# Probabilities times values: products of 64 rows for each sequence of a pair, one PSUM bank for each

## The chip, the cores and the metric

The kernel runs on one core of a Trainium2 chip. Times are device microseconds (us) of one execution; the time of a kernel is the median of its runs.

## What is computed

A gated cross-attention layer and a gated mixture of low-rank experts, on 32 sequences of 64 tokens of width 512. The part that the change touches is attention; the layer's reference, cut:

```python
x = x + jnp.tanh(g_xattn[0]) * attention(_layernorm(x), ctx, ctx, mask, wq, wk, wv, wo)
# attention, per sequence b (64 tokens), 32 query heads, 8 key/value heads of width 128
q, k = _apply_rope(query @ wq), _apply_rope(key @ wk)
v = value @ wv
raw = jnp.einsum('bhqd,bhkd->bhqk', q, k) / scale
attn = jax.nn.softmax(raw + mask, axis=-1)
out = jnp.einsum('bhqk,bhkd->bhqd', attn, v)
return out @ wo
```

The product `attn` times `v` is a sum over the 64 tokens of one sequence: half of the 128 rows of TensorE's array.

## The kernel before

Everything is one program in which each engine's order of instructions is written out by hand; semaphores connect the engines. First 64 products make keys and values of all sequences (line 839, with the layer norm of x beside them) and keep them in DRAM. Then come 64 steps (`STEPS`). A step is four sequences (`SUB_SEQS`, two pairs, `PAIRS`) with the four query heads (`GROUP`) that share one key/value head. The last four steps (`WIDE` on) are written out apart, because there are no more query projections to fill TensorE; the work of the experts (lines 811, 983, 1008, 1012) fills steps from 30 on and the end.

Precision: a float32 operand is split into a high part, rounded to the type fp32r, and a low part, the rest. A product is then three products of fp32r, high by high, low by high and high by low (`SPLIT_PRODUCTS`). Scores (line 894) are plain float32, and each such product leaves two matmul records in the trace.

TensorE's order in a step of the main loop (k from 1 to 59) is: scores of step k; `times_values(k-1)`; two query projections (`product`, line 877, six matmuls of 512 columns each); `project_out(k-1, 0)` (line 945, twelve matmuls of 512 columns); a further projection in every second step, and `turn_probs(k)`, which turns the probabilities of step k (line 905); `project_out(k-1, 1)`; one more projection.

`times_values` is what changes. It works on a pair of sequences at a time. The probabilities, turned, have the tokens of the pair on the 128 rows (sequence A on rows 0 to 63, B on 64 to 127) and head and query on the 512 columns, 256 to a pair. For each pair, into one bank (`attn[bp]`), with A's result on columns 0 to 255 and B's on 256 to 511, it issues (lines 930, 932):

- for each of the two sequences ("twins") one matmul of all 128 rows and 256 columns. `v_s[:, twin]` holds that sequence's high values on one half of the rows and its low values on the other, and `p_high[:, twin]` its high probabilities on both halves, so one matmul gives two of the three products;
- one matmul of 128 rows and 512 columns for the third product: `v_both` (high values of both) by `p_low`, a block-diagonal tile with zeros where a sequence meets the other's columns.

So a step has 6 matmuls and 6 weight loads for values, with 4 x 256 + 2 x 512 = 2,048 columns. ScalarE makes `p_high` with two copies out of PSUM (line 1621) and two copies to the other half of the rows (line 1624). VectorE makes `p_low` with two subtractions of 64 rows (line 1262). GpSimd writes the zeros of `p_low` once (line 1892). The SP queue fetches values for two steps at a time with four transfers to `v_s` and one to `v_both` (lines 649, 651).

Who waits for whom: `times_values` waits for `probs_low` and `probs_high`, for the values (`v_in`), and, for each bank, until `add_out` (line 1282, VectorE) has added that bank's earlier output projection to `acc` (semaphore `x1_added`). Each of its two banks raises `values_used` at its own last matmul. On that, `attn_high` (line 1633, ScalarE) and `attn_low` (line 1270, VectorE) split the bank into `o_s`, for which `project_out` waits.

Of the kernel before, what the change touches and what calls it, by code (L numbers as in the profile page):

```python
# [8 lines left out]
F32 = mybir.dt.float32  # L9
# [4 lines left out]
P = 128  # L14
# [29 lines left out]
TWIN_ROWS = (slice(0, SEQ), slice(SEQ, 2 * SEQ))  # L44

# [150 lines left out]
FOUR_UNTIL, ZEROS_BESIDE = 63, 63  # L196
# [96 lines left out]
def build(nc, x, ctx, mask, g_attn, g_ffn, wq, wk, wv, wo, routed_w, lora_b, table, out):  # L293
# [8 lines left out]
    with ExitStack() as stack:  # L302
# [28 lines left out]
        p_high = sb_at(base + 73728, "p_high", [P, 2, 512], F32R)  # L331
# [8 lines left out]
        p_low = sb_at(base + 131072, "p_low", [P, PAIRS, 2, GROUP * SEQ], F32R)  # L340
# [26 lines left out]
        v_both = sb("v_both", [P, 2, CHUNK_TILES, DH], F32R)  # L367
# [64 lines left out]
        zeros_set, warm_zeros = sem("zeros_set"), sem("warm_zeros")  # L432
# [130 lines left out]
        def _(e):  # L563
# [71 lines left out]
            def fetch_values(u):  # L635
                G, c, index = chunk_of(u)
                g = G % KV_HEADS
                if u >= 2:
                    e.wait_ge(values_used, PAIRS * SUBS * (u - 1))
                else:  # L640
                    e.wait_ge(x_low, 4 * len(X_PAIRS))
                if u == 0 or u == 1 or G == KV_HEADS:
                    for slot in range(VST):
                        e.wait_ge(v_stored[slot], 32 * len(range(slot, len(V_NO), VST)))
                cols = slice(g % 4 * DH, g % 4 * DH + DH)
                for twin in range(2):
                    for part in range(2):
                        rows = TWIN_ROWS[twin if part == 0 else 1 - twin]
                        e.dma_start(v_s[rows, u % 2, twin, :, :].bitcast(F32),
                                    v_kept[index, g // 4, part, TWIN_ROWS[twin], :, cols]).then_inc(v_in[u % 2], 16)  # L650
                e.dma_start(v_both[:, u % 2, :, :].bitcast(F32), v_kept[index, g // 4, 0, :, :, cols]).then_inc(v_in[u % 2], 16)
# [149 lines left out]
        def _(e):  # L801
# [79 lines left out]
            def scores(k):  # L881
                u, s = divmod(k, SUBS)
                G, c, index = chunk_of(u)
                e.wait_ge(rope_added, ROPE_NO["q", HEAD_PAIRS * G + 1, 1 if c == 0 else 3] + 1)
                e.wait_ge(k_in[u % 2], 16 * (u // 2 + 1))
                if k:
                    e.wait_ge(masked, k)
                free(score)
                for hp in range(HEAD_PAIRS):
                    for b in range(SUB_SEQS):  # L890
                        seq = s * SUB_SEQS + b
                        col = (hp * SUB_SEQS + b) * SEQ
                        two_heads = q_r[Q_SLOT[G, hp, c]][:, seq, :, :].rearrange("p h s -> p (h s)")
                        last = e.matmul(score[:, col:col + SEQ], two_heads, k_r[:, u % 2, seq * SEQ:(seq + 1) * SEQ],  # L894
                                        start=True, stop=True)
                last.then_inc(scored, 1)

            def turn_probs(k):
# [8 lines left out]
                drained[turned.name] = probs_low, 2 * k + 2  # L907

            def times_values(k, pairs=range(PAIRS)):
                u, s = divmod(k, SUBS)  # L910
                tiles = [s * PAIRS + bp for bp in range(PAIRS)]
                e.wait_ge(v_in[u % 2], 80 * (u // 2 + 1))
                e.wait_ge(probs_low, 2 * k + 2)
                e.wait_ge(probs_high, 3 * k + 3)
                cols = [slice(bp * GROUP * SEQ, (bp + 1) * GROUP * SEQ) for bp in range(PAIRS)]
                for bp in pairs:
                    if k == 0:

                        e.wait_ge(rope_added, ROPE_NO[JOBS[bp - PAIRS]] + 1)
                    elif k + 1 == STEPS:  # L920

                        if bp == 0:
                            e.wait_ge(masked, STEPS)
                        else:
                            e.wait_ge(x1_added, 2 * k - 1)
                    else:
                        e.wait_ge(x1_added, 2 * k - 1 + bp)
                    b = out_bank(k, bp)
                    for twin in range(2):
# [19 lines left out]
            def expert(what, t):  # L949
# [15 lines left out]
                elif what == "route":  # L965
# [8 lines left out]
                    elif t >= HALF_TILES + 2:  # L974

                        e.wait_ge(probs_low, 2 * STEPS)
# [113 lines left out]
            times_values(k + 1, [0])  # L1090
            scores(k + 3)
            times_values(k + 1, [1])
# [41 lines left out]
        def _(e):  # L1134
# [119 lines left out]
            def prob_low(k, *twins):  # L1254
                for twin in twins:
                    rows = TWIN_ROWS[twin]
                    e.wait_ge(probs_high, 3 * k + twin + 1)
                    if k:
                        e.wait_ge(values_used, PAIRS * k)
                    else:  # L1260
                        e.wait_ge(zeros_set, 1)
                    e.tensor_tensor(p_low[rows, :, twin, :], turned[rows, :].rearrange("p (b n) -> p b n", b=PAIRS),  # L1262
                                    p_high[rows, twin, :].bitcast(F32).rearrange("p (b n) -> p b n", b=PAIRS),
                                    ALU.subtract).then_inc(probs_low, 1)
# [134 lines left out]
            prob_low(0, 0, 1)  # L1399
            finish_key(len(JOBS) - 1)  # L1400
            for k in range(1, WIDE):
# [30 lines left out]
                if not together:  # L1432
                    prob_low(k, 0)
# [4 lines left out]
                prob_low(k, *((0, 1) if together else (1,)))  # L1438
# [25 lines left out]
            prob_low(k, 0, 1)  # L1464
# [6 lines left out]
            prob_low(k + 1, 0, 1)  # L1471
# [11 lines left out]
            prob_low(k + 2, 0, 1)  # L1483
# [9 lines left out]
            prob_low(k + 3, 0, 1)  # L1493
# [28 lines left out]
        def _(e):  # L1522
# [92 lines left out]
            def prob_high(k):  # L1615
# [184 lines left out]
        def _(e):  # L1800
# [80 lines left out]
            for n in range(len(JOBS)):  # L1881
# [7 lines left out]
                if n == ZEROS_BESIDE:  # L1889

                    e.wait_ge(rope_added, FOUR.stop)
                    e.memset(p_low[:, :, :, :].bitcast(F32), 0.0).then_inc(zeros_set, 1)
# [139 lines left out]
```

## Time and profile before

| | us |
|---|---|
| median of 3 runs (1090.81 to 1091.05) | 1091.02 |
| span of the profiled execution, first to last instruction | 1089.0 |
| TensorE matmul busy in it | 1082.4 (99%) |
| TensorE weight load busy | 919.3 (84%) |
| VectorE busy | 874.1 (80%) |
| ScalarE busy | 636.8 (58%) |
| GpSimd busy | 591.9 (54%) |

The own time of the profiled execution is not given beside its span; the median is 2.0 us above the span, which is what lies around it. Busy time of TensorE is time in which at least one matmul is under way, from its start to its modelled end. Matmuls overlap, so what a matmul costs is read from the distance of starts, not from its own duration.

### The profile page before, as it was taken

What the parts mean: (1) busy time and instruction counts of PE and PEld (TensorE: products, weight loads), DVE (VectorE), ACT (ScalarE), POOL (GpSimd) and SP (SyncE); (2) the same over time, 40 slices, a digit from 0 to 9 for tenths busy, and PEclk for the clock granted to TensorE, in tenths of its full rate; (3) what the DMA queues carried; (4) which work ended last, traced back from release to release, by engine and by line L of the source; (5) the groups of instructions that cost most, each with busy time, mean ns of one, the idle gap of its engine ahead of it and who ended that gap; (6) DMA issues with size and microseconds to landing.
All of it is one profiled execution on the core that took longest, in us unless ns stands there. A gap on an engine that the chain in (4) does not pass through costs nothing.

```text
span 1089.0 us, 17107 instructions
## 1 busy us (share of the span) xinstructions
PE 1082.4 (99%) x5640; PEld 919.3 (84%) x5640; DVE 874.1 (80%) x1423; ACT 636.8 (58%) x1112; POOL 591.9 (54%) x518
## 2 busy tenths in 40 slices
PE   9999999999999999999999999999999999999998
PEld 7888888888888888888888888888888888888886
DVE  7876657888888888888887898777777777777887
ACT  7563476586666666666655545555555555555553
POOL 5552379888877777777754433333333333333423
PEclk9999999999999999999999999999999999999999
DMA  7858964496646464646489546553535353543112
GB/s 258 273 210 336 391 220 183 155 379 201 214 155 213 155 213 156 212 156 212 141 300 380 185 136 205 177 187 111 187 110 187 112 184 114 179 116 118 40 39 78
DMA packets 106087, 206.27 MB, mean 189 GB/s; under 512 B 8849, under 2 KB 58641, under 8 KB 100113
## 3 DMA queue, kind: packets, MB, share of 16 engines
q1 hardware_dynamic: 105424, 204.40, 55.2%
q8 instruction: 47, 0.77, 0.3%
q10 hardware_dynamic: 576, 0.79, 0.2%
q14 instruction: 40, 0.32, 0.1%
HBM read 122.31 MB, written 82.84 MB: 188 GB/s over the span
## 4 chain that ended last, share of the span: by engine, by line
PE 97%; DVE 2%; DMA 0%; issue 0%; ACT 0%; DVEq 0%; SPq 0%
PE attn L945 32%; PE proj L877 28%; PE score L894 10%; PE attn L839 8%; PE score L839 4%; PE turned L839 4%; PE attn L930 3%; PE attn L932 3%; PE turned L905 3%; PE proj L811 1%; PE small L983 1%; PE small L1008 1%; PE score L983 0%; DMA near_raw<-in_ctx 0%; DVE o_s L1270 0%; DVE stats L1140 0%
## 5 line engine op out<-in xcount | busy, mean ns | idle before, releaser
L945 PE MATMUL attn<-wo_s,o_s 128*128 128x512 f32 x1524 | 374.7, 395 | 0.2 <-DVE o_s L1270 0.2
L877 PE MATMUL proj<-xB,wq_s 128*128 128x512 f32 x1344 | 332.6, 391 | 0.0
L945 PEld LDWEIGHTS attn<-wo_s,o_s 128*128 128x128 f32 x1524 | 280.9, 188 | 57.0 <-DVE o_s L1270 0.4
L877 PEld LDWEIGHTS proj<-xB,wq_s 128*128 128x128 f32 x1344 | 252.0, 188 | 51.3 <-issue 0.2
L1863 POOL TENSOR_TENSOR rot<-rot,tab 128x512 f32<-128x512 f32 x110 | 162.3, 1475 | 145.2 <-ACT rot L1584 145.0
L1633 ACT ACTIVATE o_s<-attn 128x512 fp32r<-128x512 f32 x127 | 69.3, 595 | 112.2 <-PE attn L932 112.1
L894 PEld LDWEIGHTS score<-k_r,q_r 128*128 128x128 f32 x1024 | 123.9, 191 | 5.5 <-DVE q_r L1180 0.4
L1175 DVE TENSOR_TENSOR q_r<-q_r,tab 128x512 f32<-128x512 f32 x127 | 120.9, 952 | 1.5 <-ACT x_third L1584 1.4
L894 PE MATMUL score<-k_r,q_r 128*128 128x64 f32 x1024 | 121.3, 271 | 0.0
L1605 ACT ACTIVATE copies<-proj 128x512 f32<-128x512 f32 x96 | 57.5, 599 | 78.0 <-PE proj L877 77.8
L1282 DVE SCALAR_TENSOR_TENSOR acc<-attn,gates_t,acc 128x512 f32<-128x512 f32 x127 | 94.8, 747 | 4.1 <-PE attn L945 1.2
L1863 POOL TENSOR_TENSOR rot_third<-rot_third,tab 128x512 f32<-128x512 f32 x40 | 61.3, 1533 | 57.6 <-ACT rot_third L1584 54.8
L1262 DVE TENSOR_TENSOR p_low<-turned,p_high 64x512 fp32r<-64x512 f32 x128 | 87.7, 686 | 5.2 <-ACT p_high L1621 2.8
L1621 ACT ACTIVATE p_high<-turned 64x512 fp32r<-64x512 f32 x128 | 75.6, 590 | 23.5 <-PE turned L905 21.8
L1583 ACT ACTIVATE rot<-q_r 64x512 f32<-64x512 f32 x84 | 52.4, 623 | 52.5 <-DVE q_r L1219 51.4
L1270 DVE TENSOR_TENSOR o_s<-attn,o_s 128x512 fp32r<-128x512 f32 x127 | 81.4, 680 | 1.8 <-ACT o_s L1633 1.7
L1624 ACT ACTIVATE p_high<-p_high 64x512 fp32r<-64x512 f32 x128 | 80.8, 631 | 2.8
L1219 DVE TENSOR_TENSOR q_r<-copies,proj 128x512 f32<-128x512 f32 x127 | 81.1, 678 | 0.3 <-issue 0.3
L1180 DVE TENSOR_TENSOR q_r<-q_r,rot 128x512 f32<-128x512 f32 x85 | 69.2, 814 | 6.0 <-POOL rot L1863 0.3
L1241 DVE SCALAR_TENSOR_TENSOR prob_odd<-score,mask_sb 128x512 f32<-128x512 f32 x32 | 22.1, 691 | 52.7 <-PE score L894 52.6
L1870 POOL TENSOR_TENSOR prob_odd<-prob_odd,neg_max 128x512 f32<-128x512 f32 x32 | 33.7, 1053 | 54.9 <-DVE neg_max L1246 54.0
L1870 POOL TENSOR_TENSOR prob_even<-prob_even,neg_max 128x512 f32<-128x512 f32 x32 | 33.5, 1047 | 48.5 <-DVE neg_max L1246 48.5
(269 smaller groups left out, 1681.5 us busy)
## 6 DMA issues: line engine op xcount, KB each, us to landing
wq_kept<-wq_s SPq DMA_DIRECT2D x16, 1792.0 KB, 6.3
wq_s<-wq_kept SPq DMA_DIRECT2D x16, 1792.0 KB, 8.2
v_kept<-vst SPq DMA_DIRECT2D x64, 256.0 KB, 4.3
v_s<-v_kept SPq DMA_DIRECT2D x128, 128.0 KB, 5.0
wo_kept<-wo_s SPq DMA_DIRECT2D x32, 512.0 KB, 5.7
wo_s<-wo_kept SPq DMA_DIRECT2D x32, 512.0 KB, 5.2
k_kept<-kst SPq DMA_DIRECT2D x32, 256.0 KB, 2.2
wq_raw<-in_wq SPq DMA_DIRECT2D x16, 512.0 KB, 7.8
```

The source lines that it names most:

```text
L839: last = e.matmul(b[:, :], stationary, moving, start=(kt == 0 and m == 0), stop=(kt == KT - 1 and m == 2))
L877: last = e.matmul(dst[:, :], wq_s[:, b % 2, A, s, kt, :], xB[:, B, mv, kt, :], start=(first and kt == 0 and m == 0), stop=(kt == 1 and m = ...
L894: last = e.matmul(score[:, col:col + SEQ], two_heads, k_r[:, u % 2, seq * SEQ:(seq + 1) * SEQ], start=True, stop=True)
L945: last = e.matmul(out_bank(k, bp)[:, :], o_s[:, s, bp, h, :], wo_s[n % WO_SLOTS][:, m, :], start=(h == 0 and i == 0), stop=(h == GROUP - 1 ...
L1175: e.tensor_tensor(dst, src, cos, ALU.mult).then_inc(times_cos, 1)
L1219: e.tensor_tensor(q_tile(b, j) if dst is None else dst, by_seq(copies[:, copy, :]), by_seq(proj[PRODUCTS[i][2]][:, :]), ALU.add).then_inc( ...
L1262: e.tensor_tensor(p_low[rows, :, twin, :], turned[rows, :].rearrange("p (b n) -> p b n", b=PAIRS), p_high[rows, twin, :].bitcast(F32).rear ...
L1270: e.tensor_tensor(low, src, high.bitcast(F32), ALU.subtract).then_inc(out_low, 1)
L1282: e.scalar_tensor_tensor(out=acc[:, tile, :], in0=out_bank(k, bp)[:, :], scalar=gates_t[:, 0:1], in1=acc[:, tile, :], op0=ALU.mult, op1=AL ...
L1621: e.activation(p_high[rows, twin, :], turned[rows, :], ACT.Copy).then_inc(probs_high, 1)
L1624: last = e.activation(p_high[TWIN_ROWS[1 - twin], twin, :], p_high[rows, twin, :].bitcast(F32), ACT.Copy)
L1863: e.tensor_tensor(r3, r3, sin, ALU.mult).then_inc(times_sin, 1)
```

## The change

Sequence A's three products use only rows 0 to 63 and bank `out_bank(k, 0)`; B's use only rows 64 to 127 and bank `out_bank(k, 1)`. Each is a matmul of 64 rows and 256 columns, and A's and B's alternate. The copies on the other half of the rows, the zeros and `v_both` go away. A bank now holds one sequence of each pair rather than one pair; so that a bank still holds 128 consecutive tokens for the output projection, the context and the mask are laid out on the host with the two middle sequences of each four swapped (`PLACED`), and `scores` takes its keys accordingly. Its core:

```diff
+PLACED = [2 * (b % 2) + b // 2 for b in range(SUB_SEQS)]
+PLACED_ALL = [first + b for first in range(0, BATCH, SUB_SEQS) for b in PLACED]
...
-        p_high = sb_at(base + 73728, "p_high", [P, 2, 512], F32R)
+        p_high = sb_at(base + 73728, "p_high", [P, 512], F32R)
-        p_low = sb_at(base + 131072, "p_low", [P, PAIRS, 2, GROUP * SEQ], F32R)
+        p_low = sb_at(base + 131072, "p_low", [P, 512], F32R)
...
+                for part in range(2):
+                    e.dma_start(v_s[:, u % 2, part, :, :].bitcast(F32), v_kept[index, g // 4, part, :, :, cols]).then_inc(
+                        v_in[u % 2], 16)
...
-                        seq = s * SUB_SEQS + b
+                        seq, place = s * SUB_SEQS + PLACED[b], s * SUB_SEQS + b
...
-                    b = out_bank(k, bp)
-                    for twin in range(2):
-                        e.matmul(b[:, cols[twin]], v_s[:, u % 2, twin, tiles[bp], :], p_high[:, twin, cols[bp]],
-                                 start=(twin == 0), stop=False, skip_group_check=True)
-                    e.matmul(b[:, :], v_both[:, u % 2, tiles[bp], :], p_low[:, bp].rearrange("p t n -> p (t n)"),
-                             start=False, stop=True, skip_group_check=True).then_inc(values_used, 1)
+                if k == 0:
+                    for job in JOBS[-PAIRS:]:
+                        e.wait_ge(rope_added, ROPE_NO[job] + 1)
+                elif k + 1 == STEPS:
+                    e.wait_ge(masked, STEPS)
+                    e.wait_ge(x1_added, 2 * k - 1)
+                else:
+                    e.wait_ge(x1_added, 2 * k)
+                for bp in range(PAIRS):
+                    cols = slice(bp * GROUP * SEQ, (bp + 1) * GROUP * SEQ)
+                    for i, (part, probs) in enumerate(((0, p_high), (1, p_high), (0, p_low))):
+                        for twin, rows in enumerate(TWIN_ROWS):
+                            last = e.matmul(out_bank(k, twin)[:, cols], v_s[rows, u % 2, part, sub * PAIRS + bp, :], probs[rows, cols],
+                                            start=(bp == 0 and i == 0), stop=(i == 2), skip_group_check=True)
+                            if bp + 1 == PAIRS and i == 2:
+                                last.then_inc(values_used, 1)
...
-            times_values(k + 1, [0])
             scores(k + 3)
-            times_values(k + 1, [1])
+            times_values(k + 1)
...
+                e.tensor_tensor(p_low[:, :], turned[:, :], p_high[:, :].bitcast(F32), ALU.subtract).then_inc(probs_low, 1)
...
+            mask_scores(k + 3)
             attn_low(k + 1, 0)
+            attn_low(k + 1, 1)
             expert_norms_begin(tiles_of(k)[1:])
-            mask_scores(k + 3)
             expert_norms_end(tiles_of(k)[:1])
-            attn_low(k + 1, 1)
...
-                for twin, rows in enumerate(TWIN_ROWS):
-                    e.activation(p_high[rows, twin, :], turned[rows, :], ACT.Copy).then_inc(probs_high, 1)
-                e.wait_ge(probs_high, 3 * k + 2)
-                for twin, rows in enumerate(TWIN_ROWS):
-                    last = e.activation(p_high[TWIN_ROWS[1 - twin], twin, :], p_high[rows, twin, :].bitcast(F32), ACT.Copy)
-                last.then_inc(probs_high, 1)
+                e.activation(p_high[:, :], turned[:, :], ACT.Copy).then_inc(probs_high, 1)
```

TensorE in the middle of the main loop, the end of the scores, the values and the next projection (row and column counts are the output's; `waits` names semaphores). Before:

```order
L894 MATMUL score<-k_r_58,q_r5_74 128x64 x4
L930 MATMUL attn0<-p_high_67,v_s_66 128x256 [waits probs_high,x1_added,probs_low,v_in1]
L930 MATMUL attn0<-p_high_67,v_s_66 128x256
L932 MATMUL attn0<-p_low_77,v_both_96 128x512
L930 MATMUL attn1<-p_high_67,v_s_66 128x256 [waits x1_added]
L930 MATMUL attn1<-p_high_67,v_s_66 128x256
L932 MATMUL attn1<-p_low_77,v_both_96 128x512
L877 MATMUL proj0<-xB_49,wq_s_57 128x512 [waits wq_low,copied,x_low]
```

After:

```order
L894 MATMUL score<-k_r_58,q_r5_74 128x64 x4
L926 MATMUL attn0<-p_high_67,v_s_66 128x256 [waits probs_low,x1_added,probs_high,v_in1]
L926 MATMUL attn1<-p_high_67,v_s_66 128x256
L926 MATMUL attn0<-p_high_67,v_s_66 128x256
L926 MATMUL attn1<-p_high_67,v_s_66 128x256
L926 MATMUL attn0<-p_low_77,v_s_66 128x256
L926 MATMUL attn1<-p_low_77,v_s_66 128x256
L926 MATMUL attn0<-p_high_67,v_s_66 128x256
L926 MATMUL attn1<-p_high_67,v_s_66 128x256
L926 MATMUL attn0<-p_high_67,v_s_66 128x256
L926 MATMUL attn1<-p_high_67,v_s_66 128x256
L926 MATMUL attn0<-p_low_77,v_s_66 128x256
L926 MATMUL attn1<-p_low_77,v_s_66 128x256
L877 MATMUL proj0<-xB_49,wq_s_57 128x512 [waits wq_low,copied,x_low]
```

Six matmuls became twelve, alternating between the two banks, and the second wait for `x1_added` moved to the front of the block.

TensorE in the steps written out at the end, from the output projection of step 60 to that of step 61 (`score<-` are the scores of step 63, the block or blocks of `attn<-p_high` and `attn<-p_low` are the values of step 61). Before:

```order
L945 MATMUL attn<-wo_s_60,o_s 128x512 x3
L945 MATMUL attn<-wo_s_61,o_s 128x512 x3
L945 MATMUL attn<-wo_s_62,o_s 128x512 x3
L945 MATMUL attn<-wo_s_63,o_s 128x512 x3
L930 MATMUL attn<-p_high,v_s 128x256 x2
L932 MATMUL attn<-p_low,v_both 128x512
L894 MATMUL score<-k_r,q_r_71 128x64 x4
L894 MATMUL score<-k_r,q_r_73 128x64 x4
L930 MATMUL attn<-p_high,v_s 128x256 x2
L932 MATMUL attn<-p_low,v_both 128x512
L905 MATMUL turned<-tab,prob_even 128x128 x4
```

After:

```order
L941 MATMUL attn<-wo_s_60,o_s 128x512 x3
L941 MATMUL attn<-wo_s_61,o_s 128x512 x3
L941 MATMUL attn<-wo_s_62,o_s 128x512 x3
L941 MATMUL attn<-wo_s_63,o_s 128x512 x3
L894 MATMUL score<-k_r,q_r_71 128x64 x4
L894 MATMUL score<-k_r,q_r_73 128x64 x4
L926 MATMUL attn<-p_high,v_s 128x256 x4
L926 MATMUL attn<-p_low,v_s 128x256 x2
L926 MATMUL attn<-p_high,v_s 128x256 x4
L926 MATMUL attn<-p_low,v_s 128x256 x2
L905 MATMUL turned<-tab,prob_even 128x128 x4
```

The values of bank 0, which stood ahead of the scores, now stand behind them with those of bank 1.

VectorE at the same place, from the addition of step 60's second bank (`acc`) to the split of step 61's second bank (`o_s`). Before:

```order
L1282 SCALAR_TENSOR_TENSOR acc<-attn,gates_t,acc 128x512
L1140 BN_STATS stats<-acc 128x6
L1142 BN_AGGR moments<-stats 128x2
L1144 TENSOR_SCALAR var_eps<-moments 128x1
L1270 TENSOR_TENSOR o_s<-attn,o_s 128x512
L1140 BN_STATS stats<-acc 128x6
L1142 BN_AGGR moments<-stats 128x2
L1144 TENSOR_SCALAR var_eps<-moments 128x1
L1241 SCALAR_TENSOR_TENSOR prob_odd<-score,mask_sb 128x512
L1246 TENSOR_REDUCE neg_max<-prob_odd 128x8
L1150 TENSOR_SCALAR expert_s<-acc,moments,rstd 128x512
L1270 TENSOR_TENSOR o_s<-attn,o_s 128x512
```

After:

```order
L1273 SCALAR_TENSOR_TENSOR acc<-attn,gates_t,acc 128x512
L1135 BN_STATS stats<-acc 128x6
L1137 BN_AGGR moments<-stats 128x2
L1139 TENSOR_SCALAR var_eps<-moments 128x1
L1236 SCALAR_TENSOR_TENSOR prob_odd<-score,mask_sb 128x512
L1241 TENSOR_REDUCE neg_max<-prob_odd 128x8
L1261 TENSOR_TENSOR o_s<-attn,o_s 128x512 x2
```

The mask and maximum of step 63's scores moved ahead of the split of both banks, one of them from between the two.

## Rows read from the trace of the kernel before

**Rows 1.** The page: span, busy time of each engine, and two rows of the span in 40 slices.

```profile
span 1089.0 us, 17107 instructions
...
PE 1082.4 (99%) x5640; PEld 919.3 (84%) x5640; DVE 874.1 (80%) x1423; ACT 636.8 (58%) x1112; POOL 591.9 (54%) x518
...
PE   9999999999999999999999999999999999999998
...
PEclk9999999999999999999999999999999999999999
```

**Rows 2.** What TensorE waited for: line waited for, releaser, us in total, times, longest.

```profile
PE small L1024 <- DVE warm L1343: 1.5, 1, 1.5
PE score L839 <- DVE ctxT L1170: 1.0, 1, 1.0
PE proj L811 <- DVE last_s L1150: 0.4, 1, 0.4
PE attn L945 <- DVE o_s L1270: 0.2, 1, 0.2
```

**Rows 3.** Matmul groups of TensorE by form: busy us, mean ns of one, idle before.

```profile
L945 PE MATMUL attn<-wo_s,o_s 128*128 128x512 f32 x1524 | 374.7, 395 | 0.2 <-DVE o_s L1270 0.2
...
L894 PE MATMUL score<-k_r,q_r 128*128 128x64 f32 x1024 | 121.3, 271 | 0.0
L930 PE MATMUL attn<-p_high,v_s 128*128 128x256 f32 x254 | 56.1, 302 | 0.0
L932 PE MATMUL attn<-p_low,v_both 128*128 128x512 f32 x127 | 50.3, 396 | 0.0
```

**Rows 4.** TensorE in order of time, one block of values: start us, us, then the group.

```profile
511.82 0.83 PE L894 MATMUL score<-k_r,q_r 128*128 128x64 f32 x6
512.46 0.49 PE L930 MATMUL attn<-p_high,v_s 128*128 128x256 f32 x2
512.78 0.40 PE L932 MATMUL attn<-p_low,v_both 128*128 128x512 f32 x1
513.02 0.40 PE L930 MATMUL attn<-p_high,v_s 128*128 128x256 f32 x2
513.25 0.40 PE L932 MATMUL attn<-p_low,v_both 128*128 128x512 f32 x1
513.48 0.40 PE L877 MATMUL proj<-xB,wq_s 128*128 128x512 f32 x1
```

**Rows 5.** The weight loads of the same stretch, in order of time.

```profile
511.87 0.64 PEld L894 LDWEIGHTS score<-k_r,q_r 128*128 128x128 f32 x5
512.43 0.30 PEld L930 LDWEIGHTS attn<-p_high,v_s 128*128 128x128 f32 x2
512.66 0.19 PEld L932 LDWEIGHTS attn<-p_low,v_both 128*128 128x128 f32 x1
```

**Rows 6.** TensorE in order of time: fp32r of 512 columns, transposes, float32 of 512 columns.

```profile
502.10 2.88 PE L945 MATMUL attn<-wo_s,o_s 128*128 128x512 f32 x12
...
506.19 0.60 PE L905 MATMUL turned<-tab,prob_even 128*128 128x128 f32 x4
...
1081.76 1.02 PE L1012 MATMUL small<-lora_bT,last_s 128*128 128x512 f32 x2
```

**Rows 7.** VectorE, ScalarE and TensorE around that block, in order of time.

```profile
510.18 0.75 DVE L1282 SCALAR_TENSOR_TENSOR acc<-attn,gates_t,acc 128x512 f32<-128x512 f32 x1
...
514.01 1.28 DVE L1270 TENSOR_TENSOR o_s<-attn,o_s 128x512 fp32r<-128x512 f32 x2
...
513.22 1.09 ACT L1633 ACTIVATE o_s<-attn 128x512 fp32r<-128x512 f32 x2 [0.62 <-PE attn L932]
...
516.22 1.07 PE L945 MATMUL attn<-wo_s,o_s 128*128 128x512 f32 x4
```

**Rows 8.** The groups that make `p_high` and `p_low`, by form.

```profile
L1624 ACT ACTIVATE p_high<-p_high 64x512 fp32r<-64x512 f32 x128 | 80.8, 631 | 2.8
L1621 ACT ACTIVATE p_high<-turned 64x512 fp32r<-64x512 f32 x128 | 75.6, 590 | 23.5 <-PE turned L905 21.8
...
L1262 DVE TENSOR_TENSOR p_low<-turned,p_high 64x512 fp32r<-64x512 f32 x128 | 87.7, 686 | 5.2 <-ACT p_high L1621 2.8 <-POOL p_low L1892 0.3
```

**Rows 9.** All engines in order of time in step 60, one of the last four.

```profile
1036.95 0.75 DVE L1282 SCALAR_TENSOR_TENSOR acc<-attn,gates_t,acc 128x512 f32<-128x512 f32 x1
...
1037.02 0.49 PE L930 MATMUL attn<-p_high,v_s 128*128 128x256 f32 x2
...
1037.34 0.39 PE L932 MATMUL attn<-p_low,v_both 128*128 128x512 f32 x1
...
1037.76 0.51 PE L930 MATMUL attn<-p_high,v_s 128*128 128x256 f32 x2
...
1038.34 0.60 PE L905 MATMUL turned<-tab,prob_odd 128*128 128x128 f32 x4
1038.40 1.46 DVE L1270 TENSOR_TENSOR o_s<-attn,o_s 128x512 fp32r<-128x512 f32 x2 [0.70 <-ACT o_s L1633]
...
1039.14 5.73 PE L945 MATMUL attn<-wo_s,o_s 128*128 128x512 f32 x24 [0.21 <-DVE o_s L1270]
```

More of the change, by code:

```diff
@@ L645, in fetch_values @@
                 cols = slice(g % 4 * DH, g % 4 * DH + DH)
-                for twin in range(2):
[L647 to L651, printed above, removed]
+                for part in range(2):
+                    e.dma_start(v_s[:, u % 2, part, :, :].bitcast(F32), v_kept[index, g // 4, part, :, :, cols]).then_inc(
+                        v_in[u % 2], 16)
             def store_wo(n):
@@ L890, in scores @@
                     for b in range(SUB_SEQS):
-                        seq = s * SUB_SEQS + b
+                        seq, place = s * SUB_SEQS + PLACED[b], s * SUB_SEQS + b
                         col = (hp * SUB_SEQS + b) * SEQ
                         two_heads = q_r[Q_SLOT[G, hp, c]][:, seq, :, :].rearrange("p h s -> p (h s)")
-                        last = e.matmul(score[:, col:col + SEQ], two_heads, k_r[:, u % 2, seq * SEQ:(seq + 1) * SEQ],
+                        last = e.matmul(score[:, col:col + SEQ], two_heads, k_r[:, u % 2, place * SEQ:(place + 1) * SEQ],
                                         start=True, stop=True)
@@ L906, in turn_probs @@
                 last.then_inc(probs_turned, 1)
[L907 to L927, printed above, removed]
-                    b = out_bank(k, bp)
-                    for twin in range(2):
-                        e.matmul(b[:, cols[twin]], v_s[:, u % 2, twin, tiles[bp], :], p_high[:, twin, cols[bp]],
-                                 start=(twin == 0), stop=False, skip_group_check=True)
-                    e.matmul(b[:, :], v_both[:, u % 2, tiles[bp], :], p_low[:, bp].rearrange("p t n -> p (t n)"),
-                             start=False, stop=True, skip_group_check=True).then_inc(values_used, 1)
@@ new lines, in turn_probs, with times_values @@
+                drained[turned.name] = probs_low, k + 1
+            def times_values(k):
+                u, sub = divmod(k, SUBS)
+                e.wait_ge(v_in[u % 2], 32 * (u // 2 + 1))
+                e.wait_ge(probs_high, k + 1)
+                e.wait_ge(probs_low, k + 1)
+                if k == 0:
[14 more added lines that the diff above has]
+                                last.then_inc(values_used, 1)
@@ L1252, in sum_rows, with prob_low @@
                 e.reciprocal(row_inv[:, k % 2, :], row_sum[:, k % 2, :]).then_inc(inverted, 1)
[L1254 to L1264, printed above, removed]
+            def prob_low(k):
+                e.wait_ge(probs_high, k + 1)
+                if k:
+                    e.wait_ge(values_used, PAIRS * k)
+                else:
+                    e.wait_ge(rope_added, FOUR.stop)
+                e.tensor_tensor(p_low[:, :], turned[:, :], p_high[:, :].bitcast(F32), ALU.subtract).then_inc(probs_low, 1)
             def attn_low(k, bp):
@@ L1398, in _ @@
                 q_sum(*q)
-            prob_low(0, 0, 1)
+            prob_low(0)
             finish_key(len(JOBS) - 1)
@@ L1432, in _ @@
                 if not together:
[L1433 removed]
+                    prob_low(k)
                 for q in ropes[0] if k > 2 else ():
@@ L1437, in _ @@
                 between(k, 6)
-                prob_low(k, *((0, 1) if together else (1,)))
+                if together:
+                    prob_low(k)
                 add_out(k - 1, 1)
@@ L1463, in _ @@
             add_out(k - 1, 0)
-            prob_low(k, 0, 1)
+            prob_low(k)
             sum_rows(k + 1)
@@ L1470, in _ @@
             mask_scores(k + 2)
-            prob_low(k + 1, 0, 1)
+            prob_low(k + 1)
             add_out(k, 0)
```

19 lines of the change are left out of this document (8 added, 11 removed).

## The prediction

> **What bounds the kernel now.** I read the page first: TensorE has a matmul under way for 99% of the span, at the full granted clock (2.4 GHz) in every slice [rows 1]. The waits say the same: in 1,089 us TensorE waited 3.1 us for anything [rows 2]. So only two things count: how far apart the starts of TensorE's instructions lie, and whether the change makes it wait. Durations don't tell the first, since matmuls overlap; the timeline does. Twelve matmuls of 512 columns take 2.88 us, of which the last is 0.395: (2.88 - 0.395) / 11 = 0.226 us each [rows 3, 6].
>
> One block of values runs from its first matmul at 512.46 to the next projection at 513.48: 1.02 us [rows 4]. In it a matmul of 256 columns costs 0.115 (two from 513.02 to 513.25), one of 512 about 0.235. The first pair is dearer, 0.32 instead of 0.23, because the second weight load starts late (three loads at 512.43, about 512.54 and 512.66) [rows 4, 5]. Blocks repeat to a few ns, 64 of them: 127 + 1 matmuls of line 932, two to a step [rows 3].
>
> **The price of a weight load.** This decides the case. Score matmuls have 64 columns, yet start every (0.83 - 0.27) / 5 = 0.112 us [rows 3, 4]. They are float32, where 512 columns cost 1.02 - 0.594 = 0.43 us [rows 3, 6], so 64 columns would be 0.053. What fills the other half is the load of 128 columns of weights that each has. So a stream of matmuls with a new 128 x 128 weight each can't go faster than about 0.112 us a piece, whatever their columns, and one of 256 columns (0.115) sits on that floor with its columns as well. The Trainium skill, page "TensorE: Matmul & The Clock Gate", section "LDWEIGHTS (loading the stationary operand)", says that a load goes by the columns, not by the rows: 128 / 1.2 = 107 ns. The score rows agree.
>
> **The change, part by part.**
>
> *Values on TensorE.* Six matmuls become twelve, each with its own weight load, and 2,048 columns become 12 x 256 = 3,072. If the matmuls of the two halves of the rows run side by side, with their loads, this is six pairs. I keep the late start of the first load (0.20 to the second start) and take 0.115 for each of the other five pairs: 0.20 + 0.575 = 0.78 us. Saved: 1.02 - 0.78 = 0.24 us, times 64 = 15.4 us. At best the first pair is as cheap as the others, 6 x 0.112 = 0.67, saved 0.35 x 64 = 22.4. At worst in this case another load is exposed at the block's end (0.09, as at its start): 0.87, saved 9.6. If they don't run side by side, it is the first rival. The trace of before has no matmul of fewer than 128 rows, so it can't say; these are bounds on both sides from rows 4.
>
> *ScalarE and VectorE.* Four copies of 0.59 to 0.63 us a step become one of about 0.6, so ScalarE loses some 1.8 us of 17 a step; two subtractions of 0.69 become one, as long as one of them since the columns stay 512 [rows 8]. Neither engine holds TensorE in the main loop: `p_low` and the addition that a block waits for end at 510.93, the block starts at 512.46 [rows 4, 7]. Worth 0 there. The zeros, the smaller transfers (two instead of five for two steps) and the swapped order of keys cost or give nothing: no row of TensorE's waits names them [rows 2].
>
> *Waits moved.* Both banks are now complete only at the block's end, where bank 0 used to be halfway. In the main loop the splits of both banks ended at 514.01 + 1.28 = 515.29 and `project_out` began at 516.22, behind 2.7 us of projections [rows 7]; with a block 0.24 shorter, bank 0's signal comes about 0.2 later than now and 0.9 us of slack stays. The second wait for `x1_added` moves ahead, by 0.6 us, where 1.5 us of slack is [rows 4, 7]: 0.
>
> *The last four steps* have no projections as cover. In step 60 the addition for the second bank starts at 1036.95 and ends at 1037.70; bank 0's products start at 1037.02, before it, bank 1's at 1037.76, right behind it [rows 9]. Now both start behind it, so the block ends at about 1037.76 + 0.78 = 1038.54, bank 0 complete some 0.17 later (0.28 duration less 0.115) at 1038.7. The two splits of bank 0 by 0.6 and 0.68 us give 1040.1 for `project_out`, where it was 1039.14: +1.0 us. In step 61 the scores now run ahead of both blocks and hide the addition, which gives part of it back; in steps 61 and 62 the later bank 0 costs up to 0.5 each. I take +1.0 for the end as a whole, 0 to +2 as bounds. What VectorE does there in another order is within these.
>
> **The sum:** 1089.0 - 15.4 + 1.0 = 1074.6 us of span; the median lies 2.0 above the span, so **1076.6 us**. Its own range: 1089.0 + 2.0 - 22.4 + 0 = 1068.6 to 1091.0 - 9.6 + 2 = 1083.4.
>
> **Rivals.**
>
> *One load after another (slower).* If the weight loads of the two halves share one path and queue, pairing the matmuls gives nothing, because loads alone take 0.112 each and there are twelve. The block is 0.20 + 11 x 0.115 = 1.47 us, +0.45 x 64 = +28.5, with the end 1091.0 + 28.5 + 1.0 = **1120.5 us**. The same comes out if the matmuls themselves don't overlap, as 256 columns cost 0.115. The point from which it decides: break-even is a pair at (1.02 - 0.20) / 5 = 0.164 us, so as soon as the second load adds over 0.05 to a pair, the change loses. For it: the load of line 932 starts at 512.66, together with the matmul before it (512.46 + 0.20), so loads run one ahead, not two [rows 4, 5], and the score stream shows the load path full. Against it: the halves lie on different partitions, and with all 128 rows in use each time, two ahead may simply have had no place to go.
>
> The Trainium skill, page "TensorEngine Tiling (Array Packing)", section "Tiling Modes", says that different tiles can load and multiply in parallel; and "TensorE: Matmul & The Clock Gate", section "Measured speedup vs the span model", has 3.07 times for four tiles of 32 rows at 512 columns. By those pages the first case holds; neither figure is for fp32r, whose loads are as long as the matmuls here.
>
> *A drain at each switch.* TensorE may have to empty itself when it goes from matmuls of 128 rows to those of 64 and back. The last score matmul starts 0.08 before the block and lasts 0.27 [rows 3, 4]: 0.19 of waiting. At the end a matmul of 256 columns lasts 0.28 (0.30 as a mean [rows 3]) against a spacing of 0.115: 0.165. Together 0.355 a step. The block is 0.78 + 0.355 = 1.135, +0.115 x 64 = +7.4: 1091.0 + 7.4 + 1.0 = **1099.4 us**; if the late first load falls into the drain (0.09 less), 1093.6; if the loads too wait for the drain (0.19 each, twice [rows 5]), up to 1123. For it: nothing in the trace excludes it; switches between float32 and fp32r do cost 0.09 each [rows 4, 5]. Against it: those same switches show no drain, the next matmul starts 0.08 behind one of 0.27. The Trainium skill, "TensorEngine Tiling (Array Packing)", "Tiling Modes", states this rule: a change of tiling mode drains the engine. No row here shows one.
>
> **How the numbers follow.** Side by side without a drain 0.43; one after another 0.36; side by side with a drain 0.15; something between (a pair that overlaps in part, a new wait) 0.06. Faster by over 0.2% (2.2 us, about what a measurement of this kernel can tell) is the first and a part of the last, 0.46; within 0.2% are the cheapest drain and partly overlapped pairs, 0.08; slower 0.46. The forecast is the likeliest single case, barely. The range reaches from the first case's lower end to the second's time with some room, 1069 to 1123, and leaves out about 1 in 10.
>
> **What would show each step.** Values blocks from the first matmul to the next projection: 0.78 us (first case), 1.47 (second), 1.05 to 1.15 or more with a gap at both ends and tight pairs between (third). Starts of A and B of one pair a few ns apart, or 0.11. ScalarE busy about 115 us less, VectorE about 44 less. TensorE's wait for `o_s` in step 60 grows from 0.2 us towards 1.2. A granted clock below full would be news, since no new idle time of TensorE is forecast. The forecast is wrong if loads queue, or if a switch costs more than 0.24 us.

## The result and the profile after

| | before | after |
|---|---|---|
| median, us | 1090.91 (1090.63 to 1091.05) | 1101.60 (1101.37 to 1101.80) |
| span of the profiled execution | 1089.0 | 1099.7 |
| ratio after to before | | 1.0095 (95% interval 1.008 to 1.0109) |

The change makes the kernel 10.7 us slower, where 14.4 us faster was forecast. The page of the changed kernel:

```profile
span 1099.7 us, 17456 instructions
...
PE 1092.0 (99%) x6024; PEld 918.5 (84%) x6024; DVE 833.7 (76%) x1359; ACT 525.0 (48%) x920; POOL 598.8 (54%) x517
...
PE   9999999999999999999999999999999999999998
...
PEclk9999999999999999999999999999999999999999
```

TensorE is still busy 99% of the time and its granted clock is still full, so as in [rows 1] everything hangs on the distance of starts. Less work on ScalarE and VectorE bought nothing. TensorE's groups by form, and what it waited for:

```profile
L941 PE MATMUL attn<-wo_s,o_s 128*128 128x512 f32 x1524 | 374.7, 395 | 1.6 <-DVE o_s L1261 1.6
L877 PE MATMUL proj<-xB,wq_s 128*128 128x512 f32 x1344 | 341.0, 397 | 0.0
...
L926 PE MATMUL attn<-p_high,v_s 64*128 64x256 f32 x508 | 54.5, 303 | 0.3 <-DVE acc L1273 0.3
```

```profile
PE attn L941 <- DVE o_s L1261: 1.6, 2, 0.8
...
PE attn L926 <- DVE acc L1273: 0.3, 1, 0.3
```

The group of `project_out` is as it was [rows 3]. The group of the projections (line 877), which the change does not touch, is busy 341.0 us, against 332.6 before. The waits [rows 2] grew from 0.2 to 1.6 us for `o_s`, plus 0.3 for the additions.

The block of values, to be laid beside [rows 4]: start us, us, then the group.

```profile
514.75 0.94 PE L894 MATMUL score<-k_r,q_r 128*128 128x64 f32 x7
515.63 0.50 PE L926 MATMUL attn<-p_high,v_s 64*128 64x256 f32 x4
515.97 0.28 PE L926 MATMUL attn<-p_low,v_s 64*128 64x256 f32 x2
516.08 0.40 PE L926 MATMUL attn<-p_high,v_s 64*128 64x256 f32 x4
516.31 0.28 PE L926 MATMUL attn<-p_low,v_s 64*128 64x256 f32 x2
516.52 3.06 PE L877 MATMUL proj<-xB,wq_s 128*128 128x512 f32 x12
519.42 0.84 PE L941 MATMUL attn<-wo_s,o_s 128*128 128x512 f32 x3
```

Four matmuls in 0.50 us and two in 0.28, which is what one of them takes alone: the halves run side by side, and the two matmuls of a pair start 3 ns apart in the trace. Six pairs take the place of six matmuls. But the next projection starts only at 516.52, 0.21 behind the last pair (the two of 516.31). And the weight loads of the same stretch (to be laid beside [rows 5]):

```profile
515.62 0.30 PEld L926 LDWEIGHTS attn<-p_high,v_s 64*128 64x128 f32 x4
515.85 0.19 PEld L926 LDWEIGHTS attn<-p_low,v_s 64*128 64x128 f32 x2
515.97 0.30 PEld L926 LDWEIGHTS attn<-p_high,v_s 64*128 64x128 f32 x4
516.20 0.19 PEld L926 LDWEIGHTS attn<-p_low,v_s 64*128 64x128 f32 x2
516.52 0.77 PEld L877 LDWEIGHTS proj<-xB,wq_s 128*128 128x128 f32 x4
```

No load starts between the two at 516.20 and 516.52. In the trace before, the load for the next projection began at 513.25, together with the block's last matmul [rows 4]; the loads of the kernel before:

```profile
513.13 0.19 PEld L932 LDWEIGHTS attn<-p_low,v_both 128*128 128x128 f32 x1
513.25 0.42 PEld L877 LDWEIGHTS proj<-xB,wq_s 128*128 128x128 f32 x2
```

On entry it is the same: the last score matmul starts at 514.75 + 0.94 - 0.27 = 515.42, the first load of 64 rows at 515.62.

So a step of the main loop (515.63 and its counterpart 512.46 are steps of the same kind) compares as follows:

| piece of a step | before | after | difference |
|---|---|---|---|
| last score matmul to first of values | 0.08 | 0.205 | +0.12 |
| first of values to next projection | 1.02 | 0.89 | -0.13 |
| the twelve projections, to the first of `project_out` | 2.74 | 2.90 | +0.16 |
| sum | | | +0.15 |

These pieces are the same to a few ns in nearly every step of the main loop. Over that loop (59 steps from the first block, 216.9 us, to that of step 59, at 1026.1 before and 1034.7 after) this is 8.5 us; the last steps add 2.0. Together with 0.1 ahead of the loop they are the difference of the spans, 10.6 to 10.7.

### The profile page after: what moved, and what is told of

Same layout as the page of the kernel before. It is cut to its first block, busy times and chain, and to the rows that moved or that the text cites. A ratio compares the mean times of both kernels' runs of the same rounds, so it can differ in the third digit from the quotient of the medians.

```text
span 1099.7 us, 17456 instructions
## 1 busy us (share of the span) xinstructions
PE 1092.0 (99%) x6024; PEld 918.5 (84%) x6024; DVE 833.7 (76%) x1359; ACT 525.0 (48%) x920; POOL 598.8 (54%) x517
## 4 chain that ended last, share of the span: by engine, by line
PE 97%; DVE 1%; DMA 0%; POOL 0%; ACT 0%; issue 0%; DVEq 0%; SPq 0%
PE attn L941 31%; PE proj L877 29%; PE score L894 10%; PE attn L839 8%; PE attn L926 5%; PE score L839 4%; PE turned L839 4%; PE turned L905 2%; PE proj L811 1%; PE small L1004 1%; PE small L979 1%; PE score L979 0%; DMA near_raw<-in_ctx 0%; DVE o_s L1261 0%; ACT o_s L1620 0%; PE score L811 0%
## 5 line engine op out<-in xcount | busy, mean ns | idle before, releaser
L877 PE MATMUL proj<-xB,wq_s 128*128 128x512 f32 x1344 | 341.0, 397 | 0.0
L877 PEld LDWEIGHTS proj<-xB,wq_s 128*128 128x128 f32 x1344 | 247.5, 188 | 58.8
L1850 POOL TENSOR_TENSOR rot<-rot,tab 128x512 f32<-128x512 f32 x110 | 167.8, 1526 | 111.1 <-ACT rot L1576 111.0
L1850 POOL TENSOR_TENSOR rot_third<-rot_third,tab 128x512 f32<-128x512 f32 x40 | 63.7, 1593 | 39.4 <-ACT rot_third L1576 36.1
L1236 DVE SCALAR_TENSOR_TENSOR prob_even<-score,mask_sb 128x512 f32<-128x512 f32 x32 | 22.1, 692 | 49.3 <-PE score L894 49.3
L1862 POOL TENSOR_TENSOR prob_even<-prob_even,row_inv 128x512 f32<-128x512 f32 x32 | 34.1, 1066 | 46.5 <-DVE row_inv L1247 46.5
L1796 POOL TENSOR_TENSOR rstd<-var_eps,power 128x1 f32<-128x1 f32 x32 | 18.8, 586 | 70.9 <-DVE var_eps L1139 70.9
```

The costliest lines, as they stand in the source:

```text
L877: last = e.matmul(dst[:, :], wq_s[:, b % 2, A, s, kt, :], xB[:, B, mv, kt, :], start=(first and kt == 0 and m == 0), stop=(kt == 1 and m = ...
L1850: e.tensor_tensor(r3, r3, sin, ALU.mult).then_inc(times_sin, 1)
```

## Experiments

The kernel before ran beside each group of experiments, at 1090.9 to 1091.0 us.

**Do the pairs, without the change of row count, bring what was forecast?** The values as six matmuls of all 128 rows, in the changed kernel:

```diff
-                    for i, (part, probs) in enumerate(((0, p_high), (1, p_high), (0, p_low))):
-                        for twin, rows in enumerate(TWIN_ROWS):
-                            last = e.matmul(out_bank(k, twin)[:, cols], v_s[rows, u % 2, part, sub * PAIRS + bp, :], probs[rows, cols],
+                    for i, (bank_no, part, probs) in enumerate(((0, 0, p_high), (1, 0, p_low), (bp, 1, p_high))):
+                        last = e.matmul(out_bank(k, bank_no)[:, cols], v_s[:, u % 2, part, sub * PAIRS + bp, :], probs[:, cols],
```

> The changed kernel with its block of values as six matmuls of all 128 rows and 256 columns instead of six pairs of 64 rows; it leaves out the separation of the two sequences and half of the low products, everything else (banks, waits, copies, order) stays. Theory (each change between matmuls of 128 and of 64 rows costs about 0.2 us, two in a step): the block shrinks to 0.20 + 5 x 0.115 = 0.78 us, the next projection follows at 0.12, and the time is 1091 - 15.4 + 1 to 2 = about 1077 us. Rival (what costs is something else that came with the change: the waits moved to the front of the block, the swapped keys, the end): it stays at 1088 to 1102 us.

Measured: 1079.28 us, ratio 0.9894 (0.988 to 0.9909) to the kernel before. A block in order of time:

```profile
296.74 0.37 PE L925 MATMUL attn<-p_high,v_s 128*128 128x256 f32 x1
...
297.42 0.28 PE L925 MATMUL attn<-p_high,v_s 128*128 128x256 f32 x1
297.54 0.86 PE L877 MATMUL proj<-xB,wq_s 128*128 128x512 f32 x3
```

From 296.74 to 297.54 is 0.80 us, as forecast (0.78); the next projection starts 0.12 behind the last value matmul. This kernel has the changed one's waits, its order of steps, its two banks handed on at the block's end, and as many starts; it lacks the 64 rows and, with them, the second matmul of each pair. So the pairs of 64 rows cost 1101.6 - 1079.3 = 22.3 us, 0.35 us a step. The rival falls. Whether the 64 rows or the twelve instructions and the two banks at a time are to blame, the next two runs tell.

**What does a change of row count cost by itself?** In the kernel before, far from the values and from float32, one projection matmul (or all six of one projection) is cut to rows 0 to 63:

```diff
+                        rows = slice(0, SEQ) if i in (0, 4) and (kt, m) == (1, 0) else slice(0, P)
-                        last = e.matmul(dst[:, :], wq_s[:, b % 2, A, s, kt, :], xB[:, B, mv, kt, :],
+                        last = e.matmul(dst[:, :], wq_s[rows, b % 2, A, s, kt, :], xB[rows, B, mv, kt, :],
```

> The kernel before with one matmul of 512 columns, in the middle of a run of projections, cut to rows 0 to 63 (it leaves out half of one term of that product); 64 such places, none next to float32 work or to the values. Theory (each change of row count costs 0.1 us of waiting and 0.1 us of a weight load that nothing hides): 0.33 to 0.4 us a place, 64 places: 1091 + 21 to 26 = 1112 to 1117 us. Rival (the loss belongs to the pairs, to two banks at a time, or to the change from float32 to fp32r ahead of them): under 0.1 us a place, 1091 to 1097 us.

> As one_short, but all six matmuls of that projection are cut to rows 0 to 63, in the same 64 places. Theory (the cost is for the change of row count, not for a matmul of 64 rows): as one_short, 1112 to 1117 us. Rival (each matmul of 64 rows is dearer): several times the loss of one_short.

Measured: 1117.77 us with one (ratio 1.0242, 1.0225 to 1.0259), 1119.81 with six (1.026, 1.0245 to 1.0276). That is 26.7 / 64 = 0.42 us a place for one, 28.8 / 64 = 0.45 for six. Both are a little over the 1112 to 1117 us that was expected. Six short matmuls cost hardly more than one, so the cost belongs to the place, not to the matmul. The short matmul in time (three timelines of overlapping stretches, so that the rows share matmuls):

```profile
442.55 0.83 PE L878 MATMUL proj<-xB,wq_s 128*128 128x512 f32 x2
...
442.88 0.93 PE L878 MATMUL proj<-xB,wq_s 64*128 64x512 f32 x2
...
443.31 0.73 PE L878 MATMUL proj<-xB,wq_s 128*128 128x512 f32 x2
```

A projection matmul starts 0.227 behind the one before. The short one (442.88) starts 0.33 behind its forerunner (442.55), the next (443.31) 0.43 behind it, and the one after that 0.34 behind (in the last row, 443.31 + 0.73 less its duration of 0.40 is 443.64). Over three times 0.227 that makes 0.42, the loss of a place. What TensorE's weight loader did ahead of all 64 short loads (columns: busy us, mean ns of one, idle before):

```profile
L878 PEld LDWEIGHTS proj<-xB,wq_s 64*128 64x128 f32 x64 | 11.7, 183 | 23.1 <-issue 23.1
```

23.1 / 64 = 0.36 us of idle loader ahead of each. A load for the same row count starts together with the matmul ahead of its own (the one of 513.25 above). One for another row count is held back. It starts 0.33 us behind the start of the last matmul here and 0.20 behind that of the last in the changed kernel's block, which is each time about 0.1 more than such a matmul takes in a stream (0.227, 0.115), and 0.07 ahead of its modelled end. Then comes its own 0.11, which nothing hides: the gap behind the short matmul, 0.43, holds that load and the next wait, and the gap of 0.34 holds the load for 128 rows. The rival, that the loss belongs to the pairs, to the two banks or to the float32 ahead of them, falls: none of the three is here, and the instructions are as many as before.

**Does the order within the block matter?** The same twelve matmuls, with the loop over the halves outside:

```diff
-                for bp in range(PAIRS):
-                    ...
-                        for twin, rows in enumerate(TWIN_ROWS):
+                for twin, rows in enumerate(TWIN_ROWS):
+                    for bp in range(PAIRS):
```

> The changed kernel with the same twelve matmuls of 64 rows in another order: first the six of rows 0 to 63, then the six of rows 64 to 127. Theory (only neighbours on different halves run side by side): twelve starts 0.115 apart instead of six, or eleven where the two sequences meet: +0.58 to +0.69 us a step, 1101.6 + 37 to 44 = 1138 to 1146 us. Rival (the engine finds the pairs itself, whatever their order): about 1102 us.

Measured: 1121.3 us, ratio 1.0274 (1.0258 to 1.0289), 19.7 above the changed kernel. Neither expectation: it lies halfway. The block:

```profile
563.90 0.50 PE L926 MATMUL attn<-p_high,v_s 64*128 64x256 f32 x2
564.24 0.27 PE L926 MATMUL attn<-p_low,v_s 64*128 64x256 f32 x1
564.25 0.50 PE L926 MATMUL attn<-p_high,v_s 64*128 64x256 f32 x4
564.59 0.28 PE L926 MATMUL attn<-p_low,v_s 64*128 64x256 f32 x2
564.71 0.39 PE L926 MATMUL attn<-p_high,v_s 64*128 64x256 f32 x2
564.95 0.28 PE L926 MATMUL attn<-p_low,v_s 64*128 64x256 f32 x1
565.15 0.96 PE L877 MATMUL proj<-xB,wq_s 128*128 128x512 f32 x3
```

And the first of the four of 564.25 by itself (a timeline of 564.22 to 564.30):

```profile
564.25 0.38 PE L926 MATMUL attn<-p_high,v_s 64*128 64x256 f32 x1
```

The order written is high, high, low, high, high, low for one half and then the same for the other. At 564.24 the first half's third matmul starts. The one of 564.25 starts 6 ns behind it, so it can't be of the same half; and it lasts 0.38 us, as the first matmul of a block does, whose load is exposed, where the others last 0.28. It is the other half's first. Its load runs until the first half's fourth starts (564.35), and from there the two halves go on together: the two with `p_low` of 564.59 are the first half's last, which carries the signal, and the other half's third. So the other half's first matmul started ahead of three matmuls that the program issues before it (the first half's fourth to sixth), and nine spacings of 0.115 took the place of twelve: 3 more than six pairs, 0.345 x 64 = 22 us, against 19.7 measured. From this came the next one, three of one half and three of the other in turn:

```diff
-                    for i, (part, probs) in enumerate(((0, p_high), (1, p_high), (0, p_low))):
-                        for twin, rows in enumerate(TWIN_ROWS):
+                    for twin, rows in enumerate(TWIN_ROWS):
+                        for i, (part, probs) in enumerate(((0, p_high), (1, p_high), (0, p_low))):
```

> The changed kernel with its twelve matmuls of 64 rows in the order three of the upper half, three of the lower, three upper, three lower. In one_half_then_other the lower half began together with the upper half's fourth matmul, three places ahead of its own turn, and the block took nine starts instead of twelve. Theory (the engine looks about three matmuls ahead and starts one whose half is idle): the lower half begins with or right after the first matmul, the block stays near 0.90 us and the time near 1102 us. Rival (it looks less far, or only past loads already under way): the first three run alone, three spacings of 0.115 more a step, 1102 + 22 = 1124 us.

Measured: 1102.34 us, ratio 1.0104 (1.0087 to 1.0121), 0.7 above the changed kernel. The block is the changed one's, from first to next projection 0.90 us, with the same groups of four and two:

```profile
516.27 0.51 PE L926 MATMUL attn<-p_high,v_s 64*128 64x256 f32 x4
516.61 0.28 PE L926 MATMUL attn<-p_low,v_s 64*128 64x256 f32 x2
516.73 0.40 PE L926 MATMUL attn<-p_high,v_s 64*128 64x256 f32 x4
516.96 0.28 PE L926 MATMUL attn<-p_low,v_s 64*128 64x256 f32 x2
517.17 0.50 PE L877 MATMUL proj<-xB,wq_s 128*128 128x512 f32 x1
```

The two halves start 10 ns apart, so the first matmul of the other half, fourth in the program, goes beside the first. Pairs need not be neighbours; how far ahead a partner may stand, no run here bounds.

**Is the cost fixed per block?** If a step pays once for its two changes of row count and gains by the amount of work between them, more work turns the sign. Both kernels with each block issued twice:

```diff
-                    for i, (part, probs) in enumerate(((0, p_high), (1, p_high), (0, p_low))):
+                    for i, (part, probs) in enumerate(2 * ((0, p_high), (1, p_high), (0, p_low))):
```

```diff
+                    for turn_no in range(2):
-                    for twin in range(2):
+                        for twin in range(2):
```

> The kernel before with each block of values issued twice, the second time added on top (the values come out doubled). Both theories: 64 x (4 x 0.115 + 2 x 0.235) = +60 us, 1151 us.

> The changed kernel with each block of values issued twice within one stretch of 64-row matmuls (the values come out doubled), to be compared with before_twice. Theory (a step pays 0.35 us once for its two changes of row count and gains 0.23 us for each block's worth of values): 64 x 6 x 0.115 = +44 us, 1146 us, some 5 us faster than before_twice, though the single form is 10.7 us slower. Rival (the loss grows with the number of pairs): the loss doubles, 1151 + 21 = 1172 us.

Measured: 1151.83 us for the kernel before, doubled, and 1146.09 for the changed one. The form that loses by 10.7 us on one block's work wins by 5.7 on two, as the theory of a fixed price had it. The first and last group of one doubled block and the projections behind it, before:

```profile
547.63 0.49 PE L931 MATMUL attn<-p_high,v_s 128*128 128x256 f32 x2
...
549.37 0.40 PE L933 MATMUL attn<-p_low,v_both 128*128 128x512 f32 x1
549.61 2.93 PE L877 MATMUL proj<-xB,wq_s 128*128 128x512 f32 x12
552.38 2.88 PE L947 MATMUL attn<-wo_s,o_s 128*128 128x512 f32 x12
```

and after:

```profile
545.57 0.50 PE L926 MATMUL attn<-p_high,v_s 64*128 64x256 f32 x4
...
546.98 0.29 PE L926 MATMUL attn<-p_low,v_s 64*128 64x256 f32 x2
547.20 3.01 PE L877 MATMUL proj<-xB,wq_s 128*128 128x512 f32 x12
550.05 2.88 PE L941 MATMUL attn<-wo_s,o_s 128*128 128x512 f32 x12
```

First to last group 1.74 us against 1.41, and the projections behind them 2.77 against 2.85. In the main loop alone (from block 0 to block 59, 217.0 to 1083.9 us in the one kernel, 218.2 to 1076.5 in the other) the changed form wins 8.6 us, about what it loses there with single blocks.

**What do the moved waits cost?** The kernel before with its own matmuls, but the changed kernel's waits, signals and order of the last steps:

```diff
-                        e.wait_ge(x1_added, 2 * k - 1 + bp)
+                    e.wait_ge(x1_added, 2 * k)
...
-                             start=False, stop=True, skip_group_check=True).then_inc(values_used, 1)
+                    if bp + 1 == PAIRS:
+                        last.then_inc(values_used, PAIRS)
...
-            times_values(k + 1, [0])
             scores(k + 3)
-            times_values(k + 1, [1])
+            times_values(k + 1)
```

> The kernel before, matmuls of 128 rows as they were, but with the waits and signals of the changed one: both waits for the earlier additions ahead of the block, both banks handed on at its end, and the order of the last four steps changed with them. Theory: nothing in the main loop, 1.5 to 3 us in the last four steps, 1092.5 to 1094 us. Rival 1 (the waits cost nothing anywhere): 1091 us. Rival 2 (they cost a little in each step): more than 1094 us, with the periods of the main loop longer than 12.74 and 14.12 us.

Measured: 1094.89 us, ratio 1.0037 (1.0024 to 1.005), +4.0. The main loop is unchanged (from block 0 at 217.59 to block 59 at 1026.70 it takes 809.1 us, as in the kernel before), so both rivals fall; but the waits cost more than the theory had. 0.7 us of it is ahead of the loop, where block 0 now waits for the last key (the changed kernel has no such wait in its trace, and its block 0 starts at 216.98, 0.1 later than before); about 3.5 is in the last four steps. Step 60:

```profile
1038.58 0.48 PE L927 MATMUL attn<-p_high,v_s 128*128 128x256 f32 x2 [0.65 <-DVE acc L1280]
...
1041.16 5.75 PE L944 MATMUL attn<-wo_s,o_s 128*128 128x512 f32 x24 [0.97 <-DVE o_s L1268]
```

The wait for the addition (0.65) and the wait for `o_s` (0.97) both stand in the open. In the changed kernel the same place reads (VectorE, then TensorE):

```profile
1045.16 0.75 DVE L1273 SCALAR_TENSOR_TENSOR acc<-attn,gates_t,acc 128x512 f32<-128x512 f32 x1
...
1046.06 0.50 PE L926 MATMUL attn<-p_high,v_s 64*128 64x256 f32 x4 [0.33 <-DVE acc L1273]
...
1046.97 0.66 PE L905 MATMUL turned<-tab,prob_odd 128*128 128x128 f32 x4
1048.42 5.78 PE L941 MATMUL attn<-wo_s,o_s 128*128 128x512 f32 x24 [0.79 <-DVE o_s L1261]
```

The addition ends at 1045.91, the block starts at 1046.06, and `project_out` starts at 1048.42 after 0.79 us of waiting.

**Was ScalarE's share worth something?** The kernel before without the two copies to the other half of the rows, from the second step on:

```diff
+                if k:
+                    e.activation(p_high[0:1, 1, 0:1], p_high[0:1, 0, 0:1].bitcast(F32), ACT.Copy).then_inc(probs_high, 1)
+                    return
```

> The kernel before without the two copies of high probabilities to the other half of the rows from the second step on (a copy of one element holds their place; the other halves keep the first step's numbers). It takes some 77 us of work off ScalarE. Theory (ScalarE is never waited for in the main loop): 1091 us, within 0.5. Rival (they slow TensorE by their traffic, or a wait hangs on them): 1 to 3 us faster.

Measured: 1091.09 us, ratio 1.0 (0.999 to 1.0009). Worth nothing, as TensorE never waits for it. VectorE's smaller share and the fewer transfers had no run of their own, but rows128 has them all, and its step of the main loop is 0.22 us shorter, no more than its block of values gives (0.228, less 0.007 in the projections).

## Why the prediction was wrong, step by step

- *What bounds the kernel, and the floor of 0.112 us a load.* Held. TensorE stayed at 99% and at full clock, and the pairs start 0.11 to 0.12 us apart, each with its two loads.
- *Six pairs at 0.115.* Held. The loads of the two halves run side by side as well: 12 loads went in six pairs, which decided the first rival (1120.5 us) against it. The forecast of 0.20 + 5 x 0.115 = 0.78 for the block is what six matmuls of 128 rows take (0.80 in rows128).
- *ScalarE, VectorE, the smaller transfers: 0.* Held (no_copies, rows128). ScalarE lost 111.8 us of work and VectorE 40.4, near the 115 and 44 of the forecast:

```profile
L1612 ACT ACTIVATE p_high<-turned 128x512 fp32r<-128x512 f32 x64 | 38.1, 596 | 28.8 <-PE turned L905 28.7
...
L1255 DVE TENSOR_TENSOR p_low<-turned,p_high 128x512 fp32r<-128x512 f32 x64 | 43.7, 682 | 3.2 <-ACT p_high L1612 3.2
```

- *Nothing at the block's borders.* This is the step that failed. The forecast priced the block as if it stood in a stream of its own kind and put it between matmuls of 128 rows at no price, so that 0.24 us a step would be saved; measured is 0.35 us a step for both borders, by the difference to rows128, and that turns the sign. The mechanism stood among the rivals, with 0.15, and its working (0.19 on entry, 0.165 on exit, 1099.4 us) was close in the sum. That is in part luck, for its split was off: the wait at each border is some 0.1 us (0.12 on entry, 0.09 on exit), and the load behind it is exposed (0.11 on exit; on entry the forecast had 0.09 of it already), while the rival put all into longer waits and added no load. Its last form, in which the loads wait too, was right in kind and far too dear (1123). That the switch between float32 and fp32r shows no drain was evidence about another kind of switch, and was given too much weight.
- *The projections behind the block.* Not in the forecast. They take 0.16 us more a step: about 0.105 is the exposed load behind the first of them, and the remaining 0.05 is spread over the next ten, whose starts lie mostly 0.231 to 0.240 apart for a while; in the kernel before and in rows128 only the first four or five do. This remainder does not belong to the change of row count: the doubled kernel before, all of 128 rows, has the same ten starts (its projections take 2.77, against 2.74), and the doubled changed kernel, which has the exposed load, has only the first four (2.85, against 2.90). What it hangs on is open.
- *Waits moved: 0 in the main loop.* Held (waits_moved).
- *The last four steps: +1.0 us, 0 to +2.* They gave +2.0, at the upper bound; with the old matmuls and the new waits, 3.5. The term was too small: it had one step's wait and took the others for small or hidden. The trace after has two waits of 0.8 us for `o_s`, in steps 60 and 61, one of 0.3 for the addition and a share of the borders.
- *The sum,* in spans of the profiled executions: 1089.0 - 13.0 (the main loop of rows128, 59 steps, each 0.22 shorter) + 1.7 (rows128 outside it: 0.6 ahead, which no wait in its trace explains, and 1.1 behind, the moved waits) + 21.6 (the main loop of the changed kernel over that of rows128, 0.37 a step: both borders, with the slower projections) + 0.4 (the same outside it) = 1099.7. The range of the forecast held the time only because it reached up to its rivals, and the case that came was given 0.15 where the forecast had 0.43.

The Trainium skill, page "TensorEngine Tiling (Array Packing)", section "Tiling Modes", says that changing the tiling mode drains the engine. The runs agree, and put the price at 0.35 to 0.42 us for going there and back (0.45 in six_short). The section's statement that different tiles load weights and multiply in parallel agrees too (block of the changed kernel, above).

A version better than both was not built. The doubled kernels say that values of two steps in one stretch of 64-row matmuls would pay in the main loop: each pair of steps would gain 2 x 0.228 and pay 0.35 to 0.37 once, an estimate of 30 x 0.1 = 3 us from these runs. The moved waits, 2.0 us behind the main loop in the changed kernel, would take most of that back unless they went too. It also needs four PSUM banks for values at a time, and the eight that the kernel names all have work in it. Whether both halves could write to one bank was not tried either.

## What to carry to other kernels

Matmuls of 64 rows on the two halves of the array do run side by side, weight loads included, and such a pair takes the 0.115 us of one matmul; but each stretch of them among matmuls of 128 rows costs about 0.35 to 0.45 us, so it pays only when a stretch saves more than that, here three to four starts of 0.115 us. Count the borders before the matmuls, and where TensorE is the bound, ask of each border which load can't be started early. A block-diagonal operand that keeps all matmuls at 128 rows can be the faster form although it streams zeros.

## What was not expected of the hardware

- TensorE started a matmul of the idle half ahead of three matmuls that the program issues before it (one_half_then_other; of two in three_by_three), so the order in time is not the program's across halves.
- A single matmul of 64 rows in a stream of 128 rows costs 0.42 us, nearly twice its own 0.227.
- Behind a block of values some four to ten matmuls of 512 columns start mostly 0.231 to 0.240 apart rather than 0.227, with blocks of 128 rows as with those of 64.
